# Final norm, residual and output store per expert block instead of a pass over tiles at the end

## What is computed

```python
x1 = x + gnn(layernorm(x))
t  = layernorm(x1)
logits = t @ Wr.T + br                     # [1250, 8]
top_v, top_i = top_k(logits, 2); w = softmax(top_v)
tgt2 = sum over the two experts e of  w_e * (relu(t @ W1[e].T + b1[e]) @ W2[e].T + b2[e])
y  = layernorm(t + tgt2) * gamma + beta
out = x1 + y
```

## Time and profile before

| | us |
|---|---|
| median of 3 runs (lowest, highest) | 2178.47 (2176.86, 2185.31) |
| span of the profiled execution | 2176.6 |
| TensorE busy in it | 2012.9 (92%) |
| first matmul of the expert stage | 1758.5 |
| end of the last matmul | 2113.15 |

### The profile page before, as it was taken

The page is one execution under the profiler, slowest core; times in us unless marked ns, Lnnn a source line. Parts: engine busy times, 40 slices in busy tenths (PEclk is TensorE's granted clock), DMA queues, the critical chain, the costliest instruction groups (busy, mean ns, idle before and its releaser), DMA issues. The chain is left out here.

```text
span 2176.6 us, 27961 instructions
## 1 busy us (share of the span) xinstructions
PE 2012.9 (92%) x9425; PEld 1601.7 (74%) x9425; DVE 1263.6 (58%) x2307; ACT 970.8 (45%) x1506; POOL 913.2 (42%) x799
## 2 busy tenths in 40 slices
PE   8999999999999999999999999999799589999970
PEld 6777777777777777777778677677588468778860
DVE  7589878842222222218989988888788732222216
ACT  3211122222222222229989999999544223333322
POOL 0000036555565555408777778778300022212212
PEclk9999999999999999999999999999899789999985
DMA  5323378777777777769789979999665589988449
GB/s 184 102 77 120 118 251 255 262 250 253 261 257 256 255 255 254 226 203 331 254 294 321 337 269 338 330 315 323 209 185 173 211 267 322 312 309 290 81 79 185
DMA packets 156831, 520.95 MB, mean 239 GB/s; under 512 B 30732, under 2 KB 31116, under 8 KB 154656
## 3 DMA queue, kind: packets, MB, share of 16 engines
q1 hardware_dynamic: 85872, 311.44, 41.3%
q0 software_dynamic: 70832, 207.92, 31.8%
HBM read 383.83 MB, written 154.68 MB: 247 GB/s over the span
## 5 line engine op out<-in xcount | busy, mean ns | idle before, releaser
L212 PE MATMUL psum<-w_hi,xnT_hi 128*128 128x512 f32 (+1 forms) x1592 | 422.5, 400 | 9.9 <-issue 5.0
L212 PE MATMUL psum<-w_lo,xnT_hi 128*128 128x512 f32 (+1 forms) x1592 | 420.8, 395 | 0.0
L212 PE MATMUL psum<-w_hi,xnT_lo 128*128 128x512 f32 (+1 forms) x1592 | 413.0, 394 | 0.0
L918 POOL DMA_INDIRECT sorted_rows<-acc x313 | 345.6, 1104 | 116.2 <-issue 84.5
L584 ACT ACTIVATE work<-psum 128x512 f32<-128x512 f32 (+1 forms) x150 | 89.9, 599 | 672.9 <-PE psum L212 672.9
L212 PEld LDWEIGHTS psum<-w_hi,xnT_hi 128*128 128x128 f32 (+1 forms) x1592 | 293.5, 187 | 80.9 <-issue 9.1
L212 PEld LDWEIGHTS psum<-w_lo,xnT_hi 128*128 128x128 f32 (+1 forms) x1592 | 296.7, 186 | 74.9
L212 PEld LDWEIGHTS psum<-w_hi,xnT_lo 128*128 128x128 f32 (+1 forms) x1592 | 294.7, 186 | 71.9
L1034 POOL DMA_INDIRECT w_hi<-y_rows,sort_row x168 | 230.8, 1374 | 63.2 <-issue 38.0
L1034 POOL DMA_INDIRECT w_lo<-y_rows,sort_row x164 | 216.0, 1317 | 58.5 <-issue 41.6
L1119 DVE SCALAR_TENSOR_TENSOR w_hi<-w_hi,sort_recip,y_hi 128x1024 fp32r<-128x1024 f32 x168 | 213.8, 1283 | 37.0 <-ACT y_hi L1080 32.2
(11 more groups left out here) (358 smaller groups left out, 2604.6 us busy)
## 6 DMA issues: line engine op xcount, KB each, us to landing
split_experts<-acc SPq DMA_DIRECT2D x128, 512.0 KB, 4.2
ring<-split_experts SPq DMA_DIRECT2D x16, 4096.0 KB, 15.9
w_raw<-in_wchunks SPq DMA_DIRECT2D x86, 512.0 KB, 5.2
y_rows<-work SPq DMA_DIRECT2D x144, 256.0 KB, 2.8
acc<-in_wchunks SPq DMA_DIRECT2D x64, 512.0 KB, 6.0
work<-local_rows SPq DMA_DIRECT2D x26, 384.0 KB, 4.1
sum_rows<-work SPq DMA_DIRECT2D x22, 256.0 KB, 4.6
acc<-in_bias SPq DMA_DIRECT2D x10, 512.0 KB, 5.6
```

The costliest lines, as they stand in the source:

```text
L212: i = pe.matmul(to[:rm, :], x_[:, k, m * P:m * P + rm], w_[:, s, k * HALF:(k + 1) * HALF], start=(n == 0), stop=(n == 3 * KD - 1))
L918: pool.indirect_dma_start(sorted_dram, IndirectOffsetOnAxis(ap=e_dest[:, c:c + 1], axis=0), e_rec[:, c, :], None, bounds_check=BLOCKS * P ...
```

## The change

- Routing: `picked`, `pick`, `late`, `code` mark for each slot whether its expert is the higher-numbered one of the token's two, thus the later block. The mark goes as an added 2048 (`LATE`) through the matmul that makes the lists, and becomes `late_at`: the token where the slot is late, past the end elsewhere. b2 is loaded and split here and no longer in the expert stage.
- x1 goes to a DRAM buffer of its own, and `beta` is added to it by accumulating DMAs in the z stage. `out` is only written by the last store. `sum_dram` is no longer zeroed: it starts as t plus bias term ("base"), which GpSimd stores tile by tile (`store_base`) in blocks 0 and 1 of its list, and `base_complete` waits for all of them. After that `acc` is free and holds slots: two of three for outputs, three for sums, three for x1, and gamma.
- To this end all transposes of `route_w` come first on TensorE, and the bias matmuls in blocks 0 to 2.
- Per block, `gather_x1` and `gather_sums` (two behind on GpSimd) fetch x1 and the sums of late rows, `finish` (three behind on VectorE) does norm and residual, `store_out` writes the rows. `gather_sums(b)` waits until scatter b has landed; the last block is added by VectorE and not scattered.
- The pass over tiles at the end, with its loads and stores, is gone.

The core of the diff:

```diff
@@ expert stage, gpsimd @@
-                pool.memset(o_s[:, 0, :], 0.0).then_inc(b2_zero, 1)
+                def store_base(m):
+                    pool.wait_ge(rb_added, m + 1)
+                    pool.dma_start(sum_dram[m * P:m * P + rows(m), :], acc[:rows(m), m, :])\
+                        .then_inc(base_early if m < 2 else base_stored, 16)
+                def base_complete():
+                    pool.dma_start(sum_dram[N:N + P, :], acc[:, TILES - 2, :]).then_inc(base_stored, 16)
+                    pool.wait_ge(base_early, 32)
+                    pool.wait_ge(base_stored, 16 * (TILES - 1))
+                    pool.dma_start(gamma_bc, gamma[0:1, :].to_broadcast([P, D])).then_inc(gamma_in, 16)
+                def gather_x1(b):
+                    if b >= END_SLOTS:
+                        pool.wait_ge(out_stored[b % END_SLOTS], 16 * (b // END_SLOTS))
+                    pool.indirect_dma_start(x1_rows(b), None, x1_dram, IndirectOffsetOnAxis(ap=late_at[:, b:b + 1], axis=0),
+                                            bounds_check=N - 1, oob_is_err=False).then_inc(x1_in[b % END_SLOTS], 16)
+                def gather_sums(b):
+                    pool.wait_ge(o_added, 16 * min(b + 1, LAST))
+                    if b >= END_SLOTS:
+                        pool.wait_ge(ended, b - END_SLOTS + 1)
+                    pool.indirect_dma_start(sum_rows(b), None, sum_dram, IndirectOffsetOnAxis(ap=late_at[:, b:b + 1], axis=0),
+                                            bounds_check=N - 1, oob_is_err=False).then_inc(sum_in[b % END_SLOTS], 16)
+                def store_out(b):
+                    pool.wait_ge(ended, b + 1)
+                    pool.indirect_dma_start(out, IndirectOffsetOnAxis(ap=late_at[:, b:b + 1], axis=0), x1_rows(b), None,
+                                            bounds_check=N - 1, oob_is_err=False).then_inc(out_stored[b % END_SLOTS], 16)
                 for b in range(BLOCKS_T):
-                    if b < TILES:
-                        pool.dma_start(out[b * P:b * P + rows(b), :], beta[0:1, :].to_broadcast([rows(b), D]),
-                                       accum_op=ALU.add).then_inc(x1_shifted, 16)
                     if b + TOKEN_SLOTS < BLOCKS_T:
                         gather(b + TOKEN_SLOTS)
+                    if b == 0:
+                        for m in range(6):
+                            store_base(m)
+                    if b == 1:
+                        for m in range(6, TILES):
+                            store_base(m)
+                        base_complete()
+                    if b >= 2:
+                        gather_x1(b - 2)
+                        gather_sums(b - 2)
                     if b >= 1:
                         scatter(b - 1)
-                scatter(LAST)
+                    if b >= BEHIND:
+                        store_out(b - BEHIND)
@@ expert stage, vector @@
+                def finish(b):
+                    a, o, x1 = b % 2, sum_rows(b), x1_rows(b)
...
+                    v.wait_ge(sum_in[b % END_SLOTS], GOT[b % END_SLOTS] + 16 * (b // END_SLOTS + 1))
+                    if b == LAST:
+                        v.wait_ge(o_read, 2 * b + 2)
+                        link(v.tensor_tensor(o, o, o_slot(b), ALU.add))
+                    norm_stats(v, link, o, a, P, var_ready)
+                    link(v.scalar_tensor_tensor(out=o, in0=o, scalar=aggr[:, a, 0:1], in1=gamma_bc,
+                                                op0=ALU.subtract, op1=ALU.mult))
+                    v.wait_ge(std_ready, b + 1)
+                    rstd(v, link, a, P, rs[:, a, 3:4])
...
+                    v.scalar_tensor_tensor(out=x1, in0=o, scalar=rs[:, a, 3:4], in1=x1, op0=ALU.mult, op1=ALU.add)\
+                        .then_inc(ended, 1)
                 for b in range(BLOCKS_T):
                     hidden_rows(b)
+                    for m in {0: (2, 3), 1: (6,), 2: (8,)}.get(b, ()):
+                        base_add(m)
                     if b + 1 < BLOCKS_T:
                         token_lo(b + 1)
-                    if 1 <= b <= 2 * TILES:
-                        route_add(b - 1)
+                    for m in {0: (4, 5), 1: (7,), 2: (9,)}.get(b, ()):
+                        base_add(m)
+                    if b >= BEHIND:
+                        finish(b - BEHIND)
                     hidden_lo(b)
```

More of the change, by code:

```diff
@@ L1274, in _, with shift_x1 @@
             def _(pool):
+                def shift_x1(m):
+                    pool.wait_ge(x1_stored[m % 2], 16 * (m // 2 + 1))
+                    pool.dma_start(x1_dram[m * P:m * P + rows(m), :], beta[0:1, :].to_broadcast([rows(m), D]),
+                                   accum_op=ALU.add).then_inc(x1_shifted, 16)
                 for s in range(TILES):
@@ L1279, in _ @@
                         .then_inc(zx_shifted[a], 16)
+                    if s >= 2:
+                        shift_x1(s - 2)
+                for m in range(TILES - 2, TILES):
+                    shift_x1(m)
+                pool.wait_ge(x1_shifted, 16 * TILES)
             @block.tensor
@@ L1495, in _ @@
             def _(sp):
+                sp.wait_ge(b2_zero, 1)
+                for at in B2_AT:
+                    sp.dma_start(w_raw[at:at + E, 1, :], b2).then_inc(b2_in, 16)
                 for n in range(2):
@@ L1691, in program @@
-            TAIL_ORDER = [m for lo, hi in TAIL_GROUPS for m in range(lo, hi)]
+            base_early, base_stored, gamma_in = ssem("e_base01"), ssem("e_base"), ssem("e_gamma")
+            sum_in, x1_in = landed[0:END_SLOTS], landed[END_SLOTS:2 * END_SLOTS]
+            GOT = [p + 16 * len(range(i, BLOCKS, SLOTS)) for i, p in enumerate(PLACED)]
+            out_stored = [ssem(f"f_out{i}") for i in range(END_SLOTS)]
+            var_ready, std_ready, ended = ssem("f_var"), ssem("f_std"), ssem("f_ended")
@@ L1705, in _, with o_slot, sum_rows, x1_rows @@
+            def o_slot(b):
+                return acc[:, b % O_SLOTS - 1, :] if b % O_SLOTS else o_s[:, :]
+            def sum_rows(b):
+                return acc[:, 2 + b % END_SLOTS, :]
+            def x1_rows(b):
+                return acc[:, 2 + END_SLOTS + b % END_SLOTS, :]
+            gamma_bc = acc[:, TILES - 2, :]
+            def bias_bank(m):
+                return 0 if m < 6 and m % 2 == 0 else 6
             @block.sync
             def _(sp):
-                sp.wait_ge(b2_zero, 1)
@@ L1771, in _ @@
-                for m in range(LAST_TILES[0]):
-                    pool.wait_ge(scaled, TAIL_ORDER.index(m) + 1)
-                    pool.dma_start(out[m * P:m * P + rows(m), :], acc[:rows(m), m, :], accum_op=ALU.add).then_inc(stored, 16)
-                pool.wait_ge(stored, 16 * LAST_TILES[0])
+                    if b >= BEHIND:
+                        store_out(b - BEHIND)
+                gather_x1(LAST - 1)
+                gather_sums(LAST - 1)
+                store_out(LAST - 2)
+                gather_x1(LAST)
@@ L1776, in _ @@
+                gather_sums(LAST)
+                store_out(LAST - 1)
+                store_out(LAST)
+                for i in range(END_SLOTS):
+                    pool.wait_ge(out_stored[i], 16 * len(range(i, BLOCKS_T, END_SLOTS)))
             @block.scalar
@@ L1916, in _ @@
+                for b in range(LAST - 2, BLOCKS_T):
+                    finish(b)
             @block.tensor
```

255 lines of the change are left out of this document (111 added, 144 removed).

## The result

The changed kernel took **2193.3 us** (median of 5 runs, 2189.2 to 2199.4), the kernel before 2178.5 (5 runs, 2171.5 to 2185.3). The ratio is **1.0071, with a 95% interval from 1.0051 to 1.0091**: slower by 0.7%. The forecast was 2196, slower by 0.8%.

The account below looks back on a forecast made before the run. Expert stage nearly full of TensorE work, then 63.45 us without a matmul at the end. 2176.6 - 44.5 + 7 + 20 + 30 + 5 = 2194.1 us, plus 1.9 for the median: 2196 us; range 2157 to 2230, forecast's own 2185 to 2210.

Parts of the forecast that it names:

- Removed pass: End of the kernel: the 63.45 us after the last matmul go, a tail of some 19 us replaces them; -44.5 us.
- Start of the stage: Expert stage start: transposes, bias matmuls, additions and routing work move ahead, later blocks lose bias matmuls; +7 us (3 to 11).
- The z stage: Stage before the expert stage: the beta additions move there and just fit; 0, at most +3 us.
- Base rows: Near block 4: scatter 0 and the token gather of block 5 wait for base rows to land; +20 us (8 to 35).
- Steady loop and clock: Expert blocks: finish waits for scatter then gather beside loads, +30 us (0 to 42); lower TensorE clock after halts, +5 (0 to 20).
- the working's cycle: Expert loop: hidden_lo, second, output, scatter, gather and finish close over three blocks in 46.5 us, 15.5 a block against 12.85.
- The clock term: TensorE in the loop: some ten halts drop its clock to the lower level for a while; +5 us (0 to 20).
- The cheap-gather rival: Expert loop: sums gathers beside a load land in some 6 us, loop costs 0 to 3, total 2159 us; chance 0.24.
- The rule of the Trainium skill: DMA queues: an engine takes some 9 to 17 descriptors per queue turn, so a gather of 9 passes in one turn.

Follow-up runs that it names:

- nothing_late: Changed kernel with all entries of late_at past the end, so gathers and output stores move no valid row: 2180.7 us, 1.0011 of the kernel before.
- order_four_behind: Changed kernel with finish four blocks behind, four sum slots, x1 gathered a block later, and the scatter ahead of both gathers: 2194.5 us, 1.0069 of the kernel before.
- after_few_loads: Changed kernel without the expert weight loads from the third expert on: 2144.9 us, 0.9840 of the kernel before.

## Why the prediction was right, point by point

- **Removed pass.** Predicted -44.5 us by a new tail of 19; measured -44.0, tail 19.5. The last steps (gather of sums, two finishes of 5.2 us, store) lie within 2 us of where the working put them. The last block itself gave another -2.8 us that had no term: TensorE's wait there was 2.84 us, as before the change (2.85), but this time the clock stayed up behind it.
- **Start of the stage.** Predicted +7, which is +12.5 up to block 4 and -5.7 later, when the bias matmuls are missing. Measured up to first(4): +14.3. Of it 3.7 us were there at ScalarE's last instruction of the z stage (1723.26 against 1719.55). That is no price of the change but a difference between two executions, which were 8.4 us apart at the stage's start. The routing and the start then gave 5.2 (predicted 6.8), blocks 0 to 3 3.5 (predicted 5.7). The z stage, predicted 0 to 3, gave 1.9: the last beta addition was issued at 1718.63 after a wait of 10.06 us for the x1 store, and the routing began 2.34 us after ScalarE's last instruction of the z stage (1723.26 to 1725.60) where it had been 0.42 (1719.55 to 1719.97).
- **Base rows.** Predicted +20 (8 to 35), measured 20.3 between first(4) and first(5), and the place was right: one halt at block 4, behind hidden_lo(3) and the first sums gather. The working had given 24, of which I kept 20. By its parts it was partly luck: the last base store took 9.0 us (13 to 16), scatter 0 took 16.6 (15), the empty first gather 2.1 (4.3), and the halt came in two pieces, the first at the token gather of block 5, which the working named as queued up and didn't price.
- **Steady loop and clock.** Predicted +30 and +5, less 5.7 for the bias matmuls, +29; measured +25.2. The mechanism was right, and so was the mean: first(6) to first(19) took 198.0 us, 15.2 a block (15.5 by the working's cycle of 46.5 over three), then 12.27 each. But it wasn't a steady cycle: eight of these thirteen blocks took 12.3 us and five took 16.5 to 22.5; the working had some ten halts. The division between the terms was off. Waits of TensorE rose from 6.35 us (three short ones for token gathers in the kernel before) to 27.0, so +21 and not +30. Matmuls at the lower clock behind waits rose from 2.4 to 11.5, so +9 and not +5; the bias matmuls gave -4.5 here. The clock term was mis-sized: its own rows give 1.8 us for the eight matmuls behind one halt, thus 18 for ten halts, of which it kept 5. Measured were 1.8 to 2.8 us for each of five halts, with a granted clock of 0.67 to 0.80 over the next 8.3 to 8.9 us.
- **The sum.** That the total came out 3 us from the forecast is partly luck: the waits of the loop were 9 us too high, the last block gave 3 us without a term, and the clock (4 too low), the 3.7 us ahead and some smaller ones made up for some two thirds of that.
- **The cheap-gather rival.** Refuted by the empty gathers. In the prediction I had taken 15 us for the sums gather from two token gathers; on the chain of the changed kernel it took 14.75, and 15.09 at 2034.56.
- **The rule of the Trainium skill** that was weighed ("DMA: Bandwidth & Descriptors", section "Queues, rings and completion order": round-robin by packet, some 9 to 17 descriptors of a queue in one turn) would have let a gather pass in a turn. That the engine goes round by packet agrees with these runs. The size of a turn doesn't: GpSimd's queue got one packet for each packet of the load (79 and 79), and a gather without a valid row took 13.6 us.
- **Parts without a price.** The work for late rows (x1 gather, output store) was taken as free; nothing_late shows that the late rows, of x1, sums and output together, cost some 10 us. The +30 covers them only in that its landings were taken from transfers that moved rows.

## What to carry to other kernels

Before a per-block step replaces a pass at the end, count for every transfer that it adds the time from its issue to its use in the engine's own order, and set it against a landing beside the largest load in flight, however few bytes it moves; here 12 to 17 us against 2 to 6. Look at the number of its packets rather than at its bytes. Where two such transfers follow each other, give them two blocks of distance and a slot more, and put each gather ahead of anything on its queue that waits for compute. An order that shortens one engine's cycle can lengthen another transfer's way to its user: look at the waits for each gather, one by one.

## What the runs showed of the hardware

- A gather without a single valid row took 2.1 us alone and 13.6 us when a 4 MB load was issued 0.5 us after it. In that stretch GpSimd's queue had 8.8% of the DMA engines' time for its 210 packets, the load 79.4%. While both queues had packets they took turns one for one, 79 of under 512 bytes and 79 of 32 KB in 6 us.
- A halt of TensorE costs more than itself: behind the one of 7.07 us the next eight matmuls took 3.78 us instead of 1.98, and the granted clock was 0.68 over 8.5 us. Behind the other four halts of the loop, 2.35 to 7.40 us long, 1.8 to 2.8 us were lost in the same way. The length of the halt alone doesn't decide it: in the last block the same wait of 2.85 us was followed by the lower clock in the kernel before and not in the changed kernel:

```profile
2164.43 2.08 PE L2006 MATMUL psum<-ring,hT_hi 128*128 x8 [2.84 <-DVE hT_lo L1921]
```

- Ahead of the expert stage, profiled executions of kernels that are alike up to there differ by 10 us: first(0) is at 1766.4 in order_four_behind and at 1776.5 in after_few_loads. Comparisons of a few microseconds within a stage have to go by distances within it, and the times by ratios of many runs.
